# Causal attention with relative positions: scores made twice, the second time with keys on partitions, and the output steps of four row tiles taken together

## The chip, the cores and the metric

The kernel runs on one core of a Trainium2 chip. The metric is the device time of one execution in microseconds (us), the median of several executions. A profiled execution gives the trace from which all rows below are taken.

## The reference, cut to what matters

The input is 8 sequences of 512 rows and 128 channels. After a layer norm each sequence goes through one causal attention layer with 16 heads of 8 channels, and then through six layers of windowed attention and a feed-forward layer, which the change leaves alone.

```python
scores = jnp.einsum('bhqd,bhkd->bhqk', Qh, Kh)
rel_k = rel_k_table[clip(k - q, -2, 2) + 2]
scores = (scores + jnp.einsum('bhqd,qkd->bhqk', Qh, rel_k)) / sqrt(8)
scores = jnp.where(causal, scores, -1e9)
attn = softmax(scores)
out = jnp.einsum('bhqk,bhkd->bhqd', attn, Vh) + jnp.einsum('bhqk,qkd->bhqd', attn, rel_v)
x = out @ W_o + b_o + x
```

For a causal row all keys that lie two or more places back share one table row, so the "far" scores are plain products with a shifted key bias. The key at the row itself and the one before it ("near") are computed apart, elementwise.

## The kernel before, in words

`relative_attention` gives each engine a program of its own; they meet in semaphores, and the order of the work is written out by hand. The loop is over 8 sequences `s` (a hardware loop, `Fori`). P is 128, TPS = 4 row tiles `qt` of 128 queries, NG = 4 groups of G = 4 heads, PAIRS = 8 pairs of heads.

- **Projection part of a sequence.** TensorE turns the input (L450), ScalarE copies it (`a_xT`, L510), TensorE multiplies by padded weights for queries and keys, eight chunks `c` of 512 columns (L460). ScalarE splits each into two parts (L517, L519) and VectorE joins them to `a_qkT` (L598), in which a head owns 32 partitions. Between chunks 1 to 4 `near_products` (L376, L377) makes the near keys and values, to which VectorE adds biases (L589, L590).
- **Pair part.** 32 items `n`: row tile `qt` outside, pair of heads inside. For an item TensorE writes a bf16 mask over the last 128 or 129 columns of both heads (L388) and adds the scores of 128 queries against 128(qt+1) keys, one head in 32 rows of the array, the two heads in two such row tiles (L393). VectorE takes both maxima in one reduce (`maxima`, L551) and the lesser of it and the near score (L554). ScalarE exponentiates with that as its bias (L495). TensorE turns the weights 128x128 at a time (`turn_weights`, L406), VectorE copies one head's out of PSUM (L629), ScalarE the other's (L531), and TensorE multiplies by the values (`values`, L421), a head's output in 32 columns of the array. `scores` runs two items ahead, `values` one behind.
- **Output part**, once for each row tile, spread among the pairs of the next tile: `copy_sums` (L505), `turn_sums` (L433), `normalize` (L563 to L569), `turn_output` (L439, L501), `project_output` (L443), `add_output` (L577). The last tile's stands by itself at the end of the sequence.

TensorE's stream is in order, so a matmul that waits holds back all behind it. `S` is four PSUM banks of scores, `PT` two, `O` and `M` one each. POOL forms the near products and near values (L357, L363, L368).

Of the kernel before, what the change touches and what calls it, by code (L numbers as in the profile page):

```python
# [20 lines left out]
F32 = mybir.dt.float32  # L21
# [6 lines left out]
P = 128  # L28
B, N, D = 8, 512, 128
TPS = N // P  # L30
# [21 lines left out]
C_NEAR = C_FAR + P + 1  # L52
C_PART = C_NEAR + H
NCONST = C_PART + 4


def constants():
# [24 lines left out]
    c[:, C_FAR:C_FAR + P + 1] = np.where(far, MASKED, 0.0)  # L82
    c[0, C_NEAR:C_NEAR + H] = MASKED

# [114 lines left out]
def relative_attention(nc, x, const, Wq, bq, Wk, bk, Wv, bv, Wo, bo, rel_k, rel_v, state, total, rank):  # L199
# [8 lines left out]

    with ExitStack() as ctx:
# [17 lines left out]


# [4 lines left out]
        sumsT = sb("a_sumsT", [P, NG, P])  # L233
# [4 lines left out]
        far_max = sb("a_far_max", [P, 2, H])  # L238
        nm = sb("a_nm", [P, 2, H])
        d01 = sb("a_d01", [P, 2, H])  # L240
        p01 = sb("a_p01", [P, 2, H])
        p_sum = sb("a_p_sum", [P, H])
        pv_near = sb("a_pv_near", [P, 2, D])
        probs = sb("a_probs", [P, 4, N])
        probsT = sb("a_probsT", [P, 2, 2, N])
        num = sb("a_num", [P, D])
        den = sb("a_den", [P, H])
        rden = sb("a_rden", [P, H])
        on = sb("a_on", [P, D])
        oT = sb("a_oT", [P, P])  # L250
        S = ctx.enter_context(nc.psum_tensor("a_S", [P, 4, 512], F32))
        PT = ctx.enter_context(nc.psum_tensor("a_PT", [P, 2, 512], F32))
        O = ctx.enter_context(nc.psum_tensor("a_O", [P, NG, P], F32))

# [5 lines left out]
        far_mask = rank["mask_bf"][:, C_FAR - C_MQ:C_FAR - C_MQ + P + 1]  # L260

        par_in, zeroed = sem("a_par_in"), sem("a_zeroed")
        bias_made = sem("a_bias_made")
        xa_in, xo_in = sem("a_xa_in"), sem("a_xo_in")
        seq_done = sem("a_seq_done")
        turned = sem("a_turned")
        xT_ready = sem("a_xT_ready")
        state_made = sem("a_state_made")
        proj = sem("a_proj")
        split_ready = sem("a_split_ready")  # L270
        qkT_ready = sem("a_qkT_ready")
        near_mm = sem("a_near_mm")
        near_ready = sem("a_near_ready")
        prods = sem("a_prods")
        s01_ready = sem("a_s01_ready")
        sm_ready = sem("a_sm_ready")
        scored = sem("a_scored")
        far_maxed = sem("a_far_maxed")
        nm_ready = sem("a_nm_ready")
        exped = sem("a_exped")  # L280
        flipped = sem("a_flipped")
        flip_dve, flip_act = sem("a_flip_dve"), sem("a_flip_act")
        summed = sem("a_summed")
        sums_out, sums_turned = sem("a_sums_out"), sem("a_sums_turned")
        d01_ready, p01_ready = sem("a_d01_ready"), sem("a_p01_ready")
        pool_chain = sem("a_pool_chain")
        fin = sem("a_fin")
        on_T, oT_ready, y_mm = sem("a_on_T"), sem("a_oT_ready"), sem("a_y_mm")
# [22 lines left out]
        NPAIR = TPS * PAIRS  # L311

        def region(qt):
            return (0, P, 1) if qt == 0 else (P * qt - 1, P + 1, 0)

        @block.sync
        def _(sp):
            def load_xa(s):
                sp.dma_start(xa[:], normed[:, bass.ds(s, 1), :, :].rearrange("p a t d -> p (a t) d")).then_inc(xa_in, 16)

            def load_xo(s):
                sp.dma_start(xo[:], x[bass.ds(s, 1), :, :].rearrange("a (t p) d -> p (a t) d", p=P)).then_inc(xo_in, 16)

            load_xa(0)
            load_xo(0)
            with sp.Fori(1, B) as s:

                sp.wait_ge(turned, s)
                load_xa(s)
                sp.wait_ge(seq_done, s * TPS + 1)  # L330
                load_xo(s)

        PAR = 16 * (4 * (2 + 3 * G) + 3 + 1 + 4 + 2)

        @block.gpsimd
        def _(pool):
            pool.memset(xT[:, 0:1], 0.0).then_inc(zeroed, 1)
            pool.memset(va[:, :, :, HA:HA + 1], 1.0).then_inc(zeroed, 1)
            pool.memset(va[:, :, :, HA + 1:], 0.0).then_inc(zeroed, 1)
            pool.wait_ge(par_in, PAR)  # L340
            for i in range(2):
                for r in range(3):
                    pool.tensor_tensor(kv_bias[:, i, r, :].rearrange("p (h d) -> p h d", h=H),
                                       bias[:, 1 + i, :].rearrange("p (h d) -> p h d", h=H),
                                       bc(rel[:, i, r, :], 1, H), ALU.add).then_inc(bias_made, 1)
# [3 lines left out]
            with pool.Fori(0, B) as s:  # L349
                pool.wait_ge(xT_ready, s + 1)  # L350
                pool.tensor_copy(state[:, bass.ds(s, 1), :], xT[:].unsqueeze(1)).then_inc(state_made, 1)
                pool.wait_ge(xo_in, 16 * s + 16)
                pool.tensor_tensor(xo[:], xo[:], bc(bias[:, 3, :], 1, TPS), ALU.add).then_inc(bias_made, 1)
# [4 lines left out]
                for qt in range(TPS):  # L358
                    u = s * TPS + qt

                    pool.wait_ge(p01_ready, u + 1)
                    for i in range(2):
                        pool.tensor_tensor(pv_near[:, i, :].rearrange("p (h d) -> p h d", h=H),  # L363
                                           near[:, 3 + i, qt, :].rearrange("p (h d) -> p h d", h=H),
                                           bc(p01[:, i, :], 2, HA), ALU.mult).then_inc(pool_chain, 1)
                    pool.tensor_tensor(p_sum[:], p01[:, 0, :], p01[:, 1, :], ALU.add).then_inc(pool_chain, 1)
                    pool.wait_ge(pool_chain, 4 * u + 2)
                    pool.tensor_tensor(pv_near[:, 0, :], pv_near[:, 0, :], pv_near[:, 1, :], ALU.add).then_inc(pool_chain, 1)  # L368

        @block.tensor  # L370
        def _(pe):
            def near_products(s, qt):

                if qt >= 2:
                    pe.wait_ge(near_ready, 6 * (s * TPS + qt - 1))
                pe.matmul(S[:, 2 + qt % 2, 0:3 * D], xT[:, 1 + P * qt:1 + P * (qt + 1)], w_all[:], start=True, stop=True)  # L376
                pe.matmul(PT[:, qt % 2, 0:2 * D], xT[:, P * qt:P * (qt + 1)], w_all[:, D:3 * D],  # L377
                          start=True, stop=True).then_inc(near_mm, 1)

            def scores(s, n):  # L380

                qt, pr = divmod(n, PAIRS)
                lo, width, skip = region(qt)

                if n >= 2:
                    pe.wait_ge(exped, 2 * (s * NPAIR + n - 1))
                for j in range(2):
                    pe.matmul(S[:, 2 * (n % 2) + j, lo:lo + width], rank["id_bf"][:], far_mask[:, skip:],  # L388
                              start=True, stop=False, skip_group_check=True)
                for j in range(2):  # L390
                    h = 2 * pr + j
                    g, r = h // G, 32 * (h % G)
                    last = pe.matmul(S[:, 2 * (n % 2) + j, 0:P * (qt + 1)], qkT[r:r + 32, 0, g, P * qt:P * (qt + 1)],  # L393
                                     qkT[r:r + 32, 1, g, 0:P * (qt + 1)], start=False, stop=True,
                                     skip_group_check=True)
                last.then_inc(scored, 1)

            def turn_weights(s, n):
                qt = n // PAIRS
                for j in range(2):  # L400

                    pe.wait_ge(exped, 2 * (s * NPAIR + n) + j + 1)
                    if n:
                        pe.wait_ge((flip_dve, flip_act)[j], s * NPAIR + n)
# [3 lines left out]
                    last.then_inc(flipped, 1)  # L408

            def values(s, n):  # L410
                qt, pr = divmod(n, PAIRS)
                if qt and pr == 0:
                    pe.wait_ge(sums_out, s * TPS + qt)
                for j in range(2):
                    pe.wait_ge((flip_dve, flip_act)[j], s * NPAIR + n + 1)

                for kt in range(qt + 1):
                    for j in range(2):
                        h = 2 * pr + j
                        r = 32 * (h % G)  # L420
                        last = pe.matmul(O[r:r + 32, h // G, :], va[:, kt, h, :],  # L421
# [1111 lines left out]
```

## Time and profile before

| | |
|---|---|
| runs of before | 4333.78, 4345.29, 4352.34 us, median 4345.29 |
| profiled execution | 4335.39 us, its span 4333.6 us |
| mean granted TensorE clock in it | 0.948 |
| busy in the span | TensorE 91%, VectorE 80%, ScalarE 55%, POOL 55% |

A span is the time from the first to the last instruction. A granted clock of 1.00 is TensorE at 2.4 GHz, 0.50 at 1.2 GHz. A row of the timeline gives the start, the length from the first start to the last end, the engine, the line and how many equal instructions were merged (x2). TensorE's matmuls overlap, so the distance from one start to the next tells more than the length of one. Float32 matmuls that are no transposes appear as two records each. A row of the windows gives the stretch, its length, the busy time and count of PE, PEld, DVE, ACT and POOL, the granted clock, the DMA share and GB/s.

### The profile page before, as it was taken

To read this page: it belongs to the slowest core of one execution; us is meant where nothing else is said; L and a number is where in the kernel's file an instruction comes from. 1 tells how busy PE (TensorE), PEld (TensorE's weight loads), DVE (VectorE), ACT (ScalarE), POOL (GpSimd) and SP (SyncE) were. 2 spreads that over 40 slices of the span, in tenths; PEclk is the share of its full clock that TensorE was granted. 3 is DMA by queue.
4 is the path that set the end of the run, shared out by engine and by line. 5 is a ranking of instruction groups with operands and counts; after the bars stand their busy time and mean duration, and the time that the engine had idled before them with its cause. 6 is when DMAs were issued, how large, how long until landed. Compare 5 with 4: busy or idle time off the path is not lost.

```text
span 4333.6 us, 175276 instructions
## 1 busy us (share of the span) xinstructions
PE 3951.8 (91%) x69760; PEld 3066.8 (71%) x69760; DVE 3471.0 (80%) x7786; ACT 2363.6 (55%) x4549; POOL 2364.7 (55%) x2932
## 2 busy tenths in 40 slices
PE   4999889699998899988999989999889998899998
PEld 2666656577876677865778757877667777578775
DVE  4676676699996898967899769999688986799886
ACT  2666565456663566644566535665356654365652
POOL 1110110278781677844787618777257874387770
PEclk8888888799999999999999999999999999999999
DMA  2000000022220222211222202222112221122220
GB/s 44 6 5 5 10 5 2 28 65 57 61 57 30 52 58 60 56 51 29 62 55 60 50 25 65 60 58 60 33 47 60 56 61 53 26 58 61 57 55 20
DMA packets 155083, 190.91 MB, mean 44 GB/s; under 512 B 56390, under 2 KB 77892, under 8 KB 153540
## 3 DMA queue, kind: packets, MB, share of 16 engines
q1 hardware_dynamic: 154308, 180.20, 16.5%
q8 instruction: 532, 8.72, 0.9%
q14 instruction: 243, 1.99, 0.2%
HBM read 22.54 MB, written 2.10 MB: 6 GB/s over the span
## 4 chain that ended last, share of the span: by engine, by line
PE 72%; DVE 5%; issue 3%; ACT 0%; POOL 0%; DVEq 0%; DMA 0%; SPq 0%; ACTq 0%; POOLq 0%
PE PS L989 17%; PE PS L975 9%; PE PS L1109 9%; PE PS L976 7%; PE PS L977 7%; PE PS L1013 7%; PE PS L999 7%; PE PS L1159 3%; PE PS L1103 2%; PE PS L1137 1%; PE PS L1125 1%; PE PS L1130 1%; DVE ss L1386 1%; DVE m L1391 0%; DVE t L1379 0%
## 5 line engine op out<-in xcount | busy, mean ns | idle before, releaser
L927 POOL TENSOR_TENSOR t<-t 128x1024 f32<-128x1024 f32 x384 | 908.5, 2372 | 332.0 <-DVE t L1381 331.4
L1211 ACT ACTIVATE va<-PS 128x512 f32<-128x512 f32 x384 | 230.3, 600 | 1001.1 <-PE PS L977 1000.9
L932 POOL TENSOR_TENSOR t<-t,rn 128x1024 f32<-128x1024 f32 x384 | 724.0, 1906 | 31.0 <-POOL rn L137 31.0
L975 PE MATMUL PS<-w_hi,xh 128*128 128x512 f32 x1152 | 520.2, 452 | 74.6 <-DVE xl L823 63.0
L1379 DVE TENSOR_TENSOR t<-PS,rope 128x512 f32<-128x512 f32 x768 | 523.1, 681 | 25.3 <-ACT sq L1242 24.7
L1242 ACT ACTIVATE sq<-PS 128x512 f32<-128x512 f32 x768 | 455.7, 593 | 32.9 <-PE PS L977 12.6
L977 PE MATMUL PS<-w_lo,xh 128*128 128x512 f32 x1152 | 465.2, 404 | 8.1 <-issue 8.1
L989 PE MATMUL PS<-constants,t 128*128 128x128 f32 x3072 | 449.6, 281 | 23.4 <-POOL t L932 21.3
L976 PE MATMUL PS<-w_hi,xl 128*128 128x512 f32 x1152 | 465.4, 404 | 2.0 <-issue 2.0
L1386 DVE TENSOR_REDUCE ss<-sq 128x16 f32<-128x1024 f32 x384 | 448.4, 1209 | 0.0
L989 PEld LDWEIGHTS PS<-constants,t 128*128 128x128 f32 x3072 | 358.2, 143 | 72.5 <-POOL t L932 24.6
L1109 PE MATMUL PS<-oT,w_out 128*128 128x128 f32 x3072 | 394.2, 281 | 4.3 <-ACT oT L1211 4.2
L1013 PE MATMUL PS<-vs,shared 64*32 64x65 f32 x18432 | 341.4, 229 | 40.7 <-issue 40.7
L1109 PEld LDWEIGHTS PS<-oT,w_out 128*128 128x128 f32 x3072 | 357.5, 191 | 23.1 <-ACT oT L1211 5.8
L495 ACT ACTIVATE a_probs<-a_S,a_nm 128x512 f32<-128x512 f32 (+3 forms) x512 | 241.8, 524 | 216.4 <-DVE a_nm L554 158.7
L1013 PE MATMUL PS<-va,shared 64*32 64x65 f32 x6144 | 343.3, 229 | 16.7 <-issue 16.7
L999 PEld LDWEIGHTS PS<-kT,qT 64*32 64x32 f32 x24576 | 273.1, 105 | 116.8 <-issue 93.0
L1013 PEld LDWEIGHTS PS<-vs,shared 64*32 64x32 f32 x18432 | 268.6, 107 | 113.8 <-issue 113.7
L999 PE MATMUL PS<-kT,qT 64*32 64x64 f32 x24576 | 340.2, 224 | 6.4 <-issue 5.9
L975 PEld LDWEIGHTS PS<-w_hi,xh 128*128 128x128 f32 x1152 | 221.8, 193 | 155.1 <-issue 77.0
L363 POOL TENSOR_TENSOR a_pv_near<-a_near,a_p 128x128 f32<-128x128 f32 x64 | 24.7, 408 | 556.0 <-ACT a_p L540 556.0
L1380 DVE TENSOR_TENSOR t<-PS,rope 128x256 f32<-128x256 f32 x768 | 318.8, 415 | 0.0
(162 smaller groups left out, 8830.2 us busy)
## 6 DMA issues: line engine op xcount, KB each, us to landing
vs<-va SPq DMA_DIRECT2D x768, 130.0 KB
vs<-va SPq DMA_DIRECT2D x768, 65.0 KB
t<-in_L_ffn_Wqkv SPq DMA_DIRECT2D x6, 1536.0 KB, 6.6
w_out<-in_L_ffn_Wo SPq DMA_DIRECT2D x6, 512.0 KB, 7.7
a_normed<-in_L_attn_x SPq DMA_DIRECT2D x8, 256.0 KB, 5.2
a_xa<-a_normed SPq DMA_DIRECT2D x8, 256.0 KB, 2.7
a_xo<-in_L_attn_x SPq DMA_DIRECT2D x8, 256.0 KB, 3.0
out<-total SPq DMA_DIRECT2D x8, 256.0 KB, 3.5
```

The source lines that it names most:

```text
L927: pool.tensor_tensor(mine[:, i, :], mine[:, i, :], t2[:, i, :], ALU.add).then_inc(done, 1)
L932: pool.tensor_tensor(h, h, bc(rn[:, H * i:H * (i + 1)], 2, HB), ALU.mult).then_inc(done, 1)
L975: pe.matmul(out, hi, w_hi, start=True, stop=False)
L976: pe.matmul(out, lo, w_hi, start=False, stop=False)
L977: return pe.matmul(out, hi, w_lo, start=False, stop=True)
L989: last = pe.transpose(PS[:, bank, P * j:P * (j + 1)], source(j), ident)
L999: last = pe.matmul(PS[W * w:W * (w + 1), 2 + par, 2 * W * pair:2 * W * (pair + 1)], qT[rows, pair, W * w:W * (w + 1)], kT[rows, t % 2, pai ...
L1013: last = pe.matmul(PS[W * w:W * (w + 1), (0, 2)[c] + par, HB1 * (pair % 4):HB1 * (pair % 4 + 1)], pT[rows, pair, W * w:W * (w + 1)], v, st ...
L1109: last = pe.matmul(PS[:, 4, 0:P], w_out[:, pair, :], oT[:, pair, :], start=(pair == 0), stop=(pair == PAIRS - 1))
L1242: act.activation(sq[:, i, 512 * c:512 * (c + 1)], PS[:, bank, :], ACT.Square).then_inc(done, 1)
L1379: dve.tensor_tensor(o1, src, bc(rope[:, 2 * i, t, :], 1, 8), ALU.mult)
L1386: dve.tensor_reduce(ss[:, H * i:H * (i + 1)], sq[:, i, :].rearrange("p (h d) -> p h d", h=H), X, ALU.add).then_inc(ss_made, 1)
```

## The change

1. Scores are made twice. `natural_scores` makes them as before (128 queries on partitions), but one head at a time through two PSUM banks, for the maxima alone; 64 items in a sequence. VectorE reduces each by itself.
2. For each group of four heads, `negate_maxima` takes the lesser of the negated maximum and the near score, `turn_maxima` turns these with four transposes, and VectorE copies them to a row layout (`neg_t`).
3. `turned_scores` makes the scores a second time, keys on partitions, for all later queries: tile `kt` has 512 - 128 kt columns, four heads in four banks. It writes the mask, adds the negated maximum with a product of a selecting matrix (`pick`), and adds the scores. ScalarE exponentiates it without a bias, and `values` uses the weights as they are, four heads in the four column tiles. The transposes of L406 and the copies of L629 and L531 are gone.
4. The output part is done once for a sequence, for four row tiles together, during the next sequence's projection; `near_products` come two chunks later.
5. The loops over sequences are unrolled.

```diff
-            def turn_weights(s, n):
...
-                    for kt in range(qt + 1):
-                        last = pe.transpose(PT[:, j, P * kt:P * (kt + 1)],
-                                            probs[:, 2 * (n % 2) + j, P * kt:P * (kt + 1)], ident)
...
+            def natural_scores(s, g, i):
+                qt, r = divmod(i, G)
...
+                if g or i >= 2:
+                    pe.wait_ge(far_maxed, item(s, g, i) - 1)
+                pe.matmul(S[:, i % 2, lo:lo + width], rank["id_bf"][:], far_mask[:, skip:],
+                          start=True, stop=False, skip_group_check=True)
+                pe.matmul(S[:, i % 2, 0:P * (qt + 1)], qkT[rows, 0, g, P * qt:P * (qt + 1)],
+                          qkT[rows, 1, g, 0:P * (qt + 1)], start=False, stop=True, skip_group_check=True).then_inc(nat_mm, 1)
...
+            def turned_scores(s, g, kt):
+                n = N - P * kt
+                mask = min(n, P + 1)
+                if kt == 0:
+                    pe.wait_ge(neg_turned, group(s, g) + 1)
+                for pair in range(2):
...
+                    for r in heads:
+                        pe.matmul(ST[:, r, 0:mask], rank["id_bf"][:], far_mask_t[:, 0:mask],
+                                  start=True, stop=False, skip_group_check=True)
+                    for r in heads:
+                        rows = slice(32 * r, 32 * (r + 1))
+                        pe.matmul(ST[:, r, 0:n], pick[rows, :], neg_t[rows, g % 2, P * kt:N],
+                                  start=False, stop=False, skip_group_check=True)
...
+                for i in range(ITEMS):
+                    natural_scores(s, 0, i)
+                turn_maxima(s, 0)
+                pe.wait_ge(near_ready, 6 * TPS * (s + 1))
+                for g in range(NG):
+                    for kt in range(TPS):
+                        turned_scores(s, g, kt)
+                        if kt:
+                            values(s, g, kt - 1)
+                        elif g:
+                            values(s, g - 1, TPS - 1)
+                        if g + 1 < NG:
+                            for i in CHUNKS[kt]:
+                                natural_scores(s, g + 1, i)
+                    if g + 1 < NG:
+                        turn_maxima(s, g + 1)
+                values(s, NG - 1, TPS - 1)
```

`CHUNKS` is 6, 6, 4 and 0 items. ITEMS is 16: four row tiles of four heads.

TensorE before, one item of the last row tile (`a_PT` turned weights, `a_S` scores, `a_O` sums):

```order
L406 MATMUL a_PT<-constants,a_probs 128x128 [waits a_flip_dve,a_exped]
L406 MATMUL a_PT<-constants,a_probs 128x128 x3
L402 REGISTER_ALU
L406 MATMUL a_PT<-constants,a_probs 128x128 [waits a_flip_act,a_exped]
L406 MATMUL a_PT<-constants,a_probs 128x128 x3
L386 ISA
L388 MATMUL a_S<-mask_bf,id_bf 128x129 [waits a_exped]
L388 MATMUL a_S<-mask_bf,id_bf 128x129
L393 MATMUL a_S<-a_qkT 128x512 x2
```

TensorE now, step `kt` = 1 of the first group and the start of its six natural items (`a_ST` turned scores, `a_neg_t` the maxima):

```order
L409 MATMUL a_ST<-mask_bf,id_bf 128x129 [waits a_exped]
L409 MATMUL a_ST<-mask_bf,id_bf 128x129
L413 MATMUL a_ST<-a_neg_t,a_pick 128x384 x2
L417 MATMUL a_ST<-a_qkT 128x384 x2
L426 MATMUL a_O<-a_probs,a_va 32x512 [waits a_exped]
L426 MATMUL a_O<-a_probs,a_va 32x512 x3
L385 MATMUL a_S<-mask_bf,id_bf 128x129 [waits a_far_maxed]
L387 MATMUL a_S<-a_qkT 128x256
L385 MATMUL a_S<-mask_bf,id_bf 128x129 [waits a_far_maxed]
L387 MATMUL a_S<-a_qkT 128x256
L385 MATMUL a_S<-mask_bf,id_bf 128x129 [waits a_far_maxed]
L387 MATMUL a_S<-a_qkT 128x384
```

Before, TensorE went on to the values of the pair before; now each natural item is a mask and one head's scores, and waits for the reduce of two items earlier.

VectorE before, in the pair part, where each item had a reduce of two heads and a copy:

```order
L551 TENSOR_REDUCE a_far_max<-a_S 128x2 [waits a_scored]
L554 SCALAR_TENSOR_TENSOR a_nm<-a_far_max,a_sm 128x2 [waits a_far_maxed]
L626 ISA
L629 COPY a_probsT<-a_PT 128x256 [waits a_summed,a_flipped]
L550 REGISTER_ALU
```

VectorE now, from the first group of a sequence on:

```order
L574 TENSOR_REDUCE a_far_max<-a_S 128x1 [waits a_nat_mm] x16
L579 TENSOR_REDUCE a_s<-a_prod 128x64 [waits a_prods] x2
L581 TENSOR_TENSOR a_s<-a_s,constants 128x16 [waits a_s01_ready]
L583 TENSOR_TENSOR a_sm<-a_s 128x64 [waits a_sm_ready]
L585 TENSOR_SCALAR a_sm<-a_sm 128x64 [waits a_sm_ready]
L593 SCALAR_TENSOR_TENSOR a_neg<-a_far_max,a_sm 128x16 [waits a_far_maxed,a_sm_ready]
L599 TENSOR_TENSOR a_d<-a_s,a_neg 128x4x4 [waits a_neg_made]
L599 TENSOR_TENSOR a_d<-a_s,a_neg 128x4x4
L604 CAST a_neg_t<-a_M 128x512 [waits a_neg_mm]
```

The near scores (L579 to L585), which came before the first reduce, now stand behind sixteen of them and ahead of the handing over of the first maxima.

## Rows read from the trace of the kernel before

**Rows 1.** The page: granted clock in 40 slices of 108 us, in tenths

```profile
PEclk8888888799999999999999999999999999999999
```

**Rows 2.** Windows: one sequence; then everything behind the attention (busy, counts, clock)

```profile
147.40:243.00 95.60, 87.59 (x693) 59.62 (x690) 65.45 (x161) 57.20 (x126) 10.79 (x21) 0.86 0.02 5
822.50:4333.60 3511.10, 3245.37 (x64256) 2586.20 (x64256) 2927.65 (x6388) 1905.59 (x3541) 2272.97 (x2754) 0.97 0.21 52
```

**Rows 3.** Timeline: where the parts of a sequence begin

```profile
248.15 1.06 PE L450 MATMUL a_PT<-constants,a_xa 128*128 128x128 f32 x4
...
266.66 0.34 PE L388 MATMUL a_S<-mask_bf,id_bf 128*128 128x128 bf16 x2 [2.51 <-DVE a_qkT L598]
...
339.42 0.60 ACT L505 ACTIVATE a_sumsT<-a_O 128x512 f32<-128x512 f32 x1 [1.13 <-PE a_O L421]
...
340.06 1.08 PE L433 MATMUL a_M<-constants,a_sumsT 128*128 128x36 f32 x8 [0.69 <-ACT a_sumsT L505]
...
343.73 1.06 PE L450 MATMUL a_PT<-constants,a_xa 128*128 128x128 f32 x4
```

**Rows 4.** Windows cut where the granted clock changes, one sequence

```profile
253.10:266.60 13.50, 10.34 (x29) 4.93 (x27) 11.94 (x33) 9.61 (x15) 3.65 (x3) 1.00 0.00 0
266.60:287.10 20.50, 18.95 (x101) 11.37 (x102) 12.21 (x39) 9.33 (x33) 1.36 (x4) 0.50 0.00 0
287.10:341.80 54.70, 52.97 (x550) 40.32 (x548) 40.60 (x89) 35.02 (x76) 4.09 (x12) 1.00 0.00 0
```

**Rows 5.** Timeline at the high clock: masks, scores, values, and the reduce released

```profile
318.70 0.28 PE L388 MATMUL a_S<-mask_bf,id_bf 128*128 128x129 bf16 x2
...
318.90 0.50 PE L393 MATMUL a_S<-a_qkT 32*128 32x512 f32 x2
...
319.33 0.85 PE L421 MATMUL a_O<-a_probsT,a_va 128*32 128x128 f32 x12
319.45 1.23 DVE L551 TENSOR_REDUCE a_far_max<-a_S 128x2 f32<-128x1024 f32 x1
```

**Rows 6.** Timeline at the low clock: the same places

```profile
270.50 0.47 PE L393 MATMUL a_S<-a_qkT 32*128 32x128 f32 x2
...
270.90 0.69 PE L406 MATMUL a_PT<-constants,a_probs 128*128 128x128 f32 x2
...
282.33 0.43 PE L388 MATMUL a_S<-mask_bf,id_bf 128*128 128x129 bf16 x2
...
282.69 0.58 PE L393 MATMUL a_S<-a_qkT 32*128 32x256 f32 x2
```

**Rows 7.** Groups of one shape, 50 to 823 us (busy, mean ns | idle before)

```profile
L551 DVE TENSOR_REDUCE a_far_max<-a_S 128x2 f32<-128x512 f32 x64 | 44.1, 690 | 25.1 <-PE a_S L393 24.8
L357 POOL TENSOR_TENSOR a_prod<-a_near 128x512 f32<-128x512 f32 x16 | 27.7, 1750 | 71.9 <-DVE a_va L590 71.9
L551 DVE TENSOR_REDUCE a_far_max<-a_S 128x2 f32<-128x256 f32 x64 | 27.2, 425 | 26.2 <-PE a_S L393 25.2
L495 ACT ACTIVATE a_probs<-a_S,a_nm 128x512 f32<-128x512 f32 x128 | 81.1, 684 | 50.2 <-PE a_PT L406 29.4 <-DVE a_nm L554 20.6
L629 DVE COPY a_probsT<-a_PT 128x128 f32<-128x128 f32 x64 | 18.7, 292 | 18.0 <-PE a_PT L406 17.3
```

**Rows 8.** A group of the high-clock stretch, 287.1 to 341.8 us

```profile
L406 PE MATMUL a_PT<-constants,a_probs 128*128 128x128 f32 x137 | 20.5, 281 | 0.4 <-ACT a_probsT L531 0.3
```

**Rows 9.** Timeline of VectorE: the near scores' chain

```profile
266.45 1.26 DVE L609 TENSOR_REDUCE a_s<-a_prod 128x64 f32<-128x512 f32 x2
...
268.22 0.20 DVE L617 TENSOR_SCALAR a_sm<-a_sm 128x64 f32<-128x64 f32 x1
```

**Rows 10.** Timeline of a windowed layer: matmuls in eight tiles of 64 rows and 32 columns

```profile
1500.07 0.27 PE L1013 MATMUL PS<-vs,shared 64*32 64x65 f32 x5
...
1500.21 0.25 PE L1013 MATMUL PS<-vs,shared 64*32 64x65 f32 x5
```

More of the change, by code:

```diff
@@ L310, in relative_attention, with group, item, step @@
         block = ctx.enter_context(nc.Block())
-        NPAIR = TPS * PAIRS
-        def region(qt):
-            return (0, P, 1) if qt == 0 else (P * qt - 1, P + 1, 0)
+        NC = 2 * NG
+        ITEMS = TPS * G
+        CHUNKS = (range(0, 6), range(6, 12), range(12, 16), range(16, 16))
+        PAR = 16 * (4 * (2 + 3 * G) + 3 + 1 + 4 + 2)
+        def group(s, g):
+            return s * NG + g
+        def item(s, g, i):
+            return group(s, g) * ITEMS + i
+        def step(s, g, kt):
+            return group(s, g) * TPS + kt
+        def per_head(h):
+            return h.rearrange("p (h d) -> p h d", h=H)
+        def per_tile_head(h):
+            return h.rearrange("p t (h d) -> p t h d", h=H)
         @block.sync
         def _(sp):
[L318 to L333, printed above, removed]
+            for s in range(B):
+                if s:
+                    sp.wait_ge(turned, s)
+                sp.dma_start(xa[:], normed[:, s, :, :]).then_inc(xa_in, 16)
+                if s:
+                    sp.wait_ge(seq_done, s)
+                sp.dma_start(xo[:], x[s].rearrange("(t p) d -> p t d", p=P)).then_inc(xo_in, 16)
         @block.gpsimd
         def _(pool):
-            pool.memset(xT[:, 0:1], 0.0).then_inc(zeroed, 1)
-            pool.memset(va[:, :, :, HA:HA + 1], 1.0).then_inc(zeroed, 1)
-            pool.memset(va[:, :, :, HA + 1:], 0.0).then_inc(zeroed, 1)
+            pool.memset(xT[:, 0:1], 0.0).then_inc(made, 1)
+            pool.memset(va[:, :, :, HA:HA + 1], 1.0).then_inc(made, 1)
+            pool.memset(va[:, :, :, HA + 1:], 0.0).then_inc(made, 1)
             pool.wait_ge(par_in, PAR)
@@ L378, in near_products @@
+                pe.matmul(ST[:, b, 0:2 * D], xT[:, P * qt:P * (qt + 1)], w_all[:, D:3 * D],
                           start=True, stop=True).then_inc(near_mm, 1)
[L380 to L396, printed above, removed]
@@ L410, in values @@
[L410 to L421, printed above, removed]
-                                         probsT[:, n % 2, j, P * kt:P * (kt + 1)], start=(kt == 0), stop=(kt == qt),
-                                         skip_group_check=True)
-                last.then_inc(summed, 1)
@@ new lines, in values @@
+            def values(s, g, kt):
+                n = N - P * kt
+                pe.wait_ge(exped, G * (step(s, g, kt) + 1))
+                if kt == 0 and group(s, g):
+                    pe.wait_ge(sums_out, group(s, g))
+                for r in range(G):
+                    last = pe.matmul(O[32 * r:32 * (r + 1), P * kt:N], va[:, kt, G * g + r, :], probs[:, kt % 2, r, 0:n],
+                                     start=(kt == 0), stop=(kt == TPS - 1), skip_group_check=True)
+                last.then_inc(val_mm, 1)
@@ L431, in turn_sums @@
+            def turn_sums(s):
+                pe.wait_ge(sums_out, group(s, NG))
                 keep = ident.rearrange("p (h c) -> p h c", h=G)[:, :, 0:HA + 1]
-                for g in range(NG):
-                    last = pe.matmul(M[:, 36 * g:36 * (g + 1)], sumsT[:, g, :], keep, start=True, stop=True,
-                                     skip_group_check=True)
+                for qt in range(TPS):
+                    for g in range(NG):
+                        last = pe.matmul(ST[:, qt, 36 * g:36 * (g + 1)], sumsT[:, g, P * qt:P * (qt + 1)], keep,
+                                         start=True, stop=True, skip_group_check=True)
@@ L435, in turn_sums, with turn_output @@
                 last.then_inc(sums_turned, 1)
-            def turn_output(s, qt):
-                pe.wait_ge(fin, 4 * (s * TPS + qt) + 4)
-                pe.transpose(M[:, TURNED], on[:], ident).then_inc(on_T, 1)
-            def project_output(s, qt):
-                pe.wait_ge(oT_ready, s * TPS + qt + 1)
-                pe.matmul(M[:, Y], oT[:], wo[:], start=True, stop=True).then_inc(y_mm, 1)
+            def turn_output(s):
+                pe.wait_ge(fin, 4 * s + 4)
+                for qt in range(TPS):
+                    last = pe.transpose(ST[:, qt, TURNED], on[:, qt, :], ident)
+                last.then_inc(on_T, 1)
@@ L445, in _, with project_output @@
+            def project_output(s):
+                pe.wait_ge(oT_ready, s + 1)
+                for qt in range(TPS):
+                    last = pe.matmul(ST[:, qt, Y], oT[:, qt, :], wo[:], start=True, stop=True)
+                last.then_inc(y_mm, 1)
             pe.wait_ge(bias_made, 8)
-            pe.wait_ge(zeroed, 3)
-            with pe.Fori(0, B) as s:
+            pe.wait_ge(made, 5)
+            for s in range(B):
+                if s:
+                    turn_sums(s - 1)
                 pe.wait_ge(xa_in, 16 * s + 16)
@@ L480, in _ @@
-                values(s, NPAIR - 1)
-                turn_sums(s, TPS - 1)
-                turn_output(s, TPS - 1)
-                project_output(s, TPS - 1)
+                project(s, 0)
+                if s:
+                    turn_output(s - 1)
+                project(s, 1)
+                if s:
+                    project_output(s - 1)
+                project(s, 2)
+                if s:
+                    pe.wait_ge(seq_done, s)
+                for c in range(3, NC):
+                    if c - 3 < TPS:
+                        near_products(s, c - 3)
+                    project(s, c)
@@ new lines, in turn_output, with weights @@
+            def turn_output(s):
+                act.wait_ge(on_T, s + 1)
+                act.activation(oT[:], ST[:, :, TURNED], ACT.Copy).then_inc(oT_ready, 1)
+            def weights(s, g, kt):
+                n = N - P * kt
+                for r in range(G):
+                    act.wait_ge(st_mm, G * step(s, g, kt) + r + 1)
+                    if step(s, g, kt) >= 2:
+                        act.wait_ge(val_mm, step(s, g, kt) - 1)
+                    act.activation(probs[:, kt % 2, r, 0:n], ST[:, r, 0:n], ACT.Exp, scale=SCALE_A).then_inc(exped, 1)
@@ L643, in _ @@
+            normalize(B - 1)
+            add_output(B - 1)
+            dve.wait_ge(seq_done, B)
             dve.wait_ge(state_made, B)
```

393 lines of the change are left out of this document (181 added, 212 removed).

## The prediction

> **What bounds the kernel now.** The page's clock line shows a mean of 0.8 in the first 7 slices (756 us) and 0.9 behind them [rows 1]: the attention part is the slower stretch, and the change touches nothing else. The windows give its size: a sequence lasts 95.60 us, TensorE is busy in 87.59 of them, VectorE in 65.45, ScalarE in 57.20, and what comes after the attention takes 3511.10 us, which I keep [rows 2]. The timeline then cuts a sequence [rows 3]: projection part 248.15 to 266.66 (18.5 us), pairs to 339.42 (72.8), the last output part to 343.73 (4.3). Cut at the changes of the granted clock, the pairs are two stretches [rows 4]: 20.50 us at 0.50 (1.2 GHz; all pairs of the first row tile), in which TensorE is shown busy for 18.95, and 54.70 us at 1.00 (2.4 GHz), busy 52.97. So TensorE is the bound through the pairs, and VectorE follows it. Two things decide the change: how long TensorE's new stream is, item by item with its waits, and at which clock it runs.
>
> **Prices.** At the high clock two masks take 0.20 from the first's start to the scores' start (318.70 to 318.90), two heads' scores of 512 columns 0.43 to the next matmul (318.90 to 319.33), and the reduce starts 0.55 after the scores (319.45) [rows 5]. One column a cycle is 0.053 us for 128, so scores of 384, 256 and 128 columns take 0.37, 0.31, 0.25 and one mask instead of two 0.14. In that 0.25 only 0.05 is columns: about 0.2 is paid at the change from 32-row scores to the next full-array matmul, whichever the width. VectorE needs 690 ns for 512 columns and 425 for 256; with the 292 of a 128-column copy that is 292, 425, 558, 690 [rows 7]. I take 0.06 us from the reduce's end back to TensorE.
>
> **The change, a group of four heads.** (a) *Removed*: turning the weights, 137 recorded transposes of L406 in the high stretch alone [rows 8]. 128 columns fed as float32 take twice the 0.053 of one column a cycle, about 0.11 each, so 15 of the 54.70 us. I don't subtract them but rebuild the sequence from its new parts.
>
> (b) *Natural items.* TensorE's own time is mask 0.14 plus 0.25, 0.31, 0.37, 0.43: 0.39 to 0.57, 7.7 us for the 16 of a group. But each waits for the reduce two items earlier. A bank's round is 0.14 + (0.37, 0.43, 0.49, 0.55) + (0.29, 0.43, 0.56, 0.69) + 0.06 = 0.86, 1.05, 1.24, 1.44, and two banks share it: 0.43, 0.52, 0.62, 0.72, or 9.2 us a group. VectorE in this loop is not full either: its reduces sum to 7.9. Bounds: TensorE's 7.7 below and 9.2 above.
>
> (c) *Turned scores.* A step has two pairs of heads, each two masks 0.20, two products with the maxima, and two scores 0.43, 0.37, 0.31, 0.25. The products are 32-row tiles; if the two heads run together they cost their columns alone, 0.22, 0.17, 0.11, 0.11: in all 0.85, 0.74, 0.62, 0.56 a pair, 5.5 us a group. Bound: if these don't pair, a second set of columns, some +5 us a sequence (+40).
>
> (d) *Values.* 12 records of 128 columns in two column tiles last 0.85 us to the last end [rows 5]; less a tail of about 0.2 that is 0.11 for two records side by side, 0.22 for the two records of a matmul. Four heads side by side then take 0.88, 0.66, 0.44, 0.22 for the four widths, with 4 x 0.1 for the change of shape 2.6 us a group. That four column tiles do run together I take from the windowed layers: ten records of 65 columns between 1500.07 and 1500.21 [rows 10], 0.014 each, less than the 0.027 that one alone needs for its columns. Bound: two at a time, +2.2 a group, +70 in all.
>
> (e) *Handing over the maxima.* Four transposes at 0.11, 0.2 to VectorE, a copy of 512 (0.69) and the return: 1.4 us. TensorE has nothing else in its stream there (`CHUNKS` ends with 0), so it is on the path. Scores of the next group wait for it. In the first group the near scores stand ahead of it on VectorE: 266.45 to 268.42 is this chain today (two reduces of 1.26, then three small ones to 268.22 + 0.20) [rows 9], so 2.0 + 0.2 for the negation + 1.4 = 3.6. POOL's products before it, 2 x 1.75 [rows 7], are made during the natural items and are hidden.
>
> The group is 9.2 + 5.5 + 2.6 + 1.4 = 18.7, three times 56.1. Ahead stand the first natural items and their handing over, 9.2 + 3.6 = 12.8; the fourth group has no natural items, 5.5 + 2.6 + 0.5 = 8.6.
>
> (f) *Output part.* `turn_sums` has 32 records, 8 of which last 1.08 today [rows 3]; less the tail, 0.11 each at the high clock: 3.6. With the copy ahead of it (0.65), the projection part 18.5 and 1.0 for the output's chain inside it: 23.7. Today projection and output part are 22.8.
>
> (g) *At nothing.* ScalarE: four exponentials of 684 ns [rows 7] are 2.7 us in the widest step, and a step with its natural items lasts over 4. POOL's chain for the near values starts in the last group and has the output's projection to run under. Loads and the later `near_products` lie under other work; unrolling I put at 0, gain at most 1 us a sequence.
>
> **Sum at the high clock**: 12.8 + 56.1 + 8.6 + 23.7 = 101.2 us, 5.6 more than 95.6, eight times 45: 4335 + 45 = 4380.
>
> **The clock.** Today it falls as TensorE idles before the first pairs (266.66 follows a wait of 2.51 [rows 3]) and stays at 0.50 for all the 128-column pairs [rows 4]. The change puts at this very place sixteen items that carry a mask and one head's scores in 0.43 to 0.72 us where a pair carries two, with TensorE waiting in each, and then a wait of 3.6 us. At low clock two masks take 0.36 (282.33 to 282.69) and a score of 128 columns 0.40 (270.50 to 270.90) [rows 6]; with 0.107 for each further 128 an item is 0.65, 0.76, 0.86, 0.97, 13.0 a group instead of 9.2. Turned steps become 9.7 (+4.2), values +2.3, handing over +0.5: a group +10.8, the first natural part +4.3, the last group +6.6. In the pair part this is 0 (high throughout) to 43.3 (low throughout). I choose low for the first natural part and one and a half groups, because today's clock needed 20.5 us of steady pairs to come back, while the natural stretches, up to 13 us a group at the low clock, cut the steady work up; it is a choice between ends far apart: 4.3 + 16.2 = 20.5, so 121.7 a sequence. 26.1 x 8 = 209: 4335 + 209 = 4544 for the profile, 4550 with the 10 by which the median stands above it.
>
> The Trainium skill, page "TensorE: Matmul & The Clock Gate", Part 4, says that PE-mode transposes do not count as activity for the clock gate. Here 137 of them ran at a granted 1.00 between 287.10 and 341.80, between other matmuls [rows 8]. By the rule alone the removal would help the clock, which is the second case below; the row doesn't decide.
>
> **Rivals.** *High clock throughout* (4380 to 4390, 0.13): for it, the turned steps are denser streams than today's pairs. Against it, [rows 4]'s low stretch was shown 92% busy.
>
> *Low throughout the pair part* (101.2 + 43.3 = 144.5, 4335 + 391 = 4726, 0.15): the natural items recur in three of four groups and could hold it down each time.
>
> *Not slower* (4297, 0.08): the items go at VectorE's pace. If a reduce started as the one before ended, 0.29 to 0.69, the 64 items would take less: with a mean of 0.41 for 0.57, 10.4 us less a sequence. At the high clock 101.2 - 10.4 = 90.8, 38 us below today. Below 0.48 us a mean item (0.57 - 5.6/64, rounded) this decides. Against it: two banks and the 0.55 from score to reduce [rows 5].
>
> *Another price* of the bounds, at the mixed clock (0.02 faster or same; the rest is slower).
>
> The Trainium skill, page "TensorEngine Tiling (Array Packing)", Key Properties, says that a change of tiling mode drains TensorE. The change alternates full array, 32-row and 32-column tiles far oftener. The page gives no time; this trace gives about 0.2 behind scores and 0.1 behind values, and these are already in (b) to (d).
>
> **How the numbers follow.** Mixed clock 0.62, high 0.13, low 0.15, not slower 0.08, others 0.02. The predicted time is that of the likeliest, 4550. The range takes the high case's 4380 and the low one's 4720; what lies beyond them is the not-slower case, the low case's upper half and part of the bounds. A measurement here tells about 0.5% (22 us) from no change, so: slower 0.91, same 0.04, faster 0.05.
>
> **What would show it.** Right: a period near 121 us; natural items spaced 0.43 to 0.72 (or 0.65 to 0.97 at granted 0.50), waiting for L574; four values of 512 columns within 0.9 us; 3.6 us idle before the first turned step; a clock of 0.50 from the first natural item into the second group; TensorE's busy share lower, VectorE's about the same. Wrong: a clock that rises within the first natural part (then 4380), natural items without waits, values in two turns (+70), products with the maxima one after another (+40), or exponentials as the releaser of turned steps, which I priced at nothing.

## The result, and the profile after

The changed kernel takes 4755.66 us (median of 4 runs, 4753.74 to 4757.11) against 4348.82 of before: ratio 1.094, 95% interval 1.091 to 1.097. That is above the range of 4380 to 4720; it is 30 us above the second rival (low clock throughout the pair part, 4726).

The page's clock line of the changed kernel, to be held against [rows 1]; a slice is 119 us:

```profile
PEclk7555555555699999999999999999999999999999
```

The windows of one sequence, of the stretch at the high clock in it, and of the one at the low clock that follows (columns as in [rows 2]):

```profile
343.60:490.90 147.30, 135.10 (x547) 66.68 (x548) 51.37 (x124) 38.57 (x87) 9.04 (x8) 0.56 0.01 4
349.80:366.90 17.10, 12.38 (x44) 6.70 (x42) 11.11 (x35) 9.38 (x14) 3.45 (x3) 1.00 0.10 32
366.90:496.60 129.70, 122.22 (x502) 59.54 (x502) 40.10 (x88) 29.19 (x73) 5.59 (x6) 0.50 0.00 1
```

A sequence lasts 147.3 us instead of 95.6, and eight times 51.7 is 414, nearly all of the 421 us by which the spans of the two profiles differ (4754.5 against 4333.6; the medians differ by 407). TensorE has 547 recorded matmuls in it where it had 693, is busy for 135.1 instead of 87.6, and VectorE and ScalarE are needed less (51.4 and 38.6). The granted clock is 1.00 in 17.1 us of the projection part alone; it falls 1.4 us after the first natural item (366.90), which had followed 3.23 us of idling, and stays at 0.50 for 129.7 us, through the next sequence's first projections.

The timeline of TensorE, from the first natural items to the next sequence:

```profile
365.50 0.23 PE L385 MATMUL a_S<-mask_bf,id_bf 128*128 128x128 bf16 x1 [3.23 <-DVE a_qkT L568]
365.66 0.32 PE L387 MATMUL a_S<-a_qkT 32*128 32x128 f32 x1
365.91 0.23 PE L385 MATMUL a_S<-mask_bf,id_bf 128*128 128x128 bf16 x1
...
380.33 1.12 PE L395 MATMUL a_M<-constants,a_neg 128*128 128x128 f32 x4 [2.89 <-DVE a_neg L593]
382.28 0.38 PE L409 MATMUL a_ST<-mask_bf,id_bf 128*128 128x129 bf16 x2 [0.83 <-issue]
382.58 0.79 PE L413 MATMUL a_ST<-a_neg_t,a_pick 32*128 32x512 f32 x2
383.18 0.63 PE L417 MATMUL a_ST<-a_qkT 32*128 32x512 f32 x2
383.74 0.40 PE L409 MATMUL a_ST<-mask_bf,id_bf 128*128 128x129 bf16 x2
...
388.42 0.29 PE L385 MATMUL a_S<-mask_bf,id_bf 128*128 128x129 bf16 x1
388.64 0.58 PE L387 MATMUL a_S<-a_qkT 32*128 32x256 f32 x1
389.15 0.40 PE L409 MATMUL a_ST<-mask_bf,id_bf 128*128 128x129 bf16 x2
...
391.68 1.94 PE L426 MATMUL a_O<-a_probs,a_va 128*32 128x512 f32 x8
393.55 0.29 PE L385 MATMUL a_S<-mask_bf,id_bf 128*128 128x129 bf16 x1
...
410.45 0.40 PE L409 MATMUL a_ST<-mask_bf,id_bf 128*128 128x129 bf16 x2 [0.79 <-DVE a_neg_t L604]
...
439.23 0.40 PE L409 MATMUL a_ST<-mask_bf,id_bf 128*128 128x129 bf16 x2 [0.79 <-DVE a_neg_t L604]
...
468.01 0.40 PE L409 MATMUL a_ST<-mask_bf,id_bf 128*128 128x129 bf16 x2 [0.79 <-DVE a_neg_t L604]
...
483.61 7.04 PE L435 MATMUL a_ST<-constants,a_sumsT 128*128 128x36 f32 x32 [0.72 <-ACT a_sumsT L524]
490.46 1.09 PE L458 MATMUL a_S<-constants,a_xa 128*128 128x128 f32 x4
```

Scores and products with the maxima leave one record for each matmul, so `x2` is two heads; the values (`x8` is four heads), the sums, the projections and the unread float32 matmuls of e4, e5 and e9 below leave two.

The reader is to see three things. Between the handings over, TensorE never idles for VectorE: a 256-column item takes 0.73 us (388.42 to 389.15) by TensorE's own time, not by the reduce. The groups follow each other 28.8 us apart (410.45, 439.23, 468.01). And in the pair part all scores and all products with the maxima are over 32 rows of the array (`32*128`); masks, values and the turning of the maxima are over 128. Summed over the records of the three groups from 382.3 to 468.0, matmuls over 32 rows are 57.4 of 98.7 us; in the stretch of before that ran at 1.00, 287.1 to 341.8, they are 9.4 of 62.8.

### The profile page after: what moved, and what is told of

Read it like the earlier page. It is cut to its first block, busy times and chain, and to the rows that moved or that the text cites. A ratio compares the mean times of both kernels' runs of the same rounds, so it can differ in the third digit from the quotient of the medians.

```text
span 4754.5 us, 168913 instructions
## 1 busy us (share of the span) xinstructions
PE 4330.7 (91%) x68608; PEld 3120.8 (66%) x68608; DVE 3359.6 (71%) x7475; ACT 2213.3 (47%) x4238; POOL 2345.4 (49%) x2836
## 4 chain that ended last, share of the span: by engine, by line
PE 66%; DVE 5%; issue 3%; ACT 0%; POOL 0%; DVEq 0%; DMA 0%; SPq 0%; ACTq 0%; POOLq 0%
PE PS L994 15%; PE PS L980 8%; PE PS L1114 8%; PE PS L982 7%; PE PS L981 7%; PE PS L1018 7%; PE PS L1004 6%; PE PS L1164 3%; PE PS L1108 2%; PE PS L1142 1%; PE PS L1130 1%; PE PS L1135 1%; DVE ss L1391 1%; DVE m L1396 0%; DVE t L1384 0%
## 5 line engine op out<-in xcount | busy, mean ns | idle before, releaser
L574 DVE TENSOR_REDUCE a_far_max<-a_S 128x1 f32<-128x384 f32 (+3 forms) x512 | 251.6, 491 | 443.3 <-PE a_S L387 442.5
L518 ACT ACTIVATE a_probs<-a_ST 128x256 f32<-128x256 f32 (+3 forms) x512 | 196.0, 434 | 735.7 <-PE a_ST L417 735.6
L1247 ACT ACTIVATE sq<-PS 128x512 f32<-128x512 f32 x768 | 455.6, 593 | 35.4 <-PE PS L982 15.4
L356 POOL TENSOR_TENSOR a_pv_near<-a_near,a_p 128x512 f32<-128x512 f32 x16 | 16.8, 1072 | 862.3 <-ACT a_p L545 862.3
```

What stands on the lines that cost most here:

```text
L1247: act.activation(sq[:, i, 512 * c:512 * (c + 1)], PS[:, bank, :], ACT.Square).then_inc(done, 1)
```

## The experiments

The first theory was the prediction's: the clock is lost in TensorE's waits and thin natural items. Its rivals were the unrolling, and the added work whatever the clock. The first four runs ask that. Where an expectation says theory A, it is that matmuls over 32 rows don't hold the clock, or that full-array columns do; it came up after e3. Ratios, with their 95% intervals, are to the kernel before, run on the same chip.

**e1: the kernel before, unrolled.**

```diff
-            with pe.Fori(0, B) as s:
+            for s in range(0, B):
```

(the same on the other engines)

> The kernel before with its loops over sequences unrolled and nothing else. Clock theory (the loss is TensorE at 1.2 GHz through the pair part): no change, 4335 to 4350 us. Rival theory (unrolled code costs, or moves the work at the seams): up to 1% slower; were the whole loss from it, 4750.

4351.24 us, ratio 1.006 (1.004 to 1.008). So unrolling accounts for some 0.6 of the 9.4 percent (at most 0.8), and that goes with the clock: with TensorE's order unchanged, its windows show a low stretch of 27.3 us at the first pairs, where [rows 4] has 20.5. Others have up to 34.5 us, and all but the first have periods (from one sequence's start to the next's) of 97 to 102 us for 95.6.

```profile
362.40:389.70 27.30, 25.67 (x139) 16.40 (x140) 14.99 (x49) 12.13 (x39) 1.36 (x4) 0.50 0.00 1
```

**e2 and e3: the changed kernel with unread matmuls around its first natural items, and behind all natural items.** The `fill(1)` stands behind each natural item, in e2 of the first group alone.

```diff
+                    pe.matmul(M[:, 0:width], rank["id_bf"][:], rank["mask_bf"][:, 0:width], start=True, stop=True, ...)
...
+                fill(24)
                 pe.wait_ge(qkT_ready, NC * (s + 1))
...
+                fill(1)
...
+                fill(24)
                 turn_maxima(s, 0)
```

> The changed kernel, with matmuls whose result nobody reads (256 bf16 columns, 0.11 us each at 2.4 GHz) put into TensorE's waits around the first group's natural items: 24 in the wait for the last queries and keys, one behind each of the 16 items, 24 in the wait for the first maxima. Clock theory: the clock, which falls at the first natural items, stays at 1.00 there; if the three later groups of natural items can hold it, the period is near 101 us (total near 4385); if they lose it by themselves it falls at the first chunk of the second group's items and the total is 4690 to 4740. Rival theory (32-row matmuls don't carry the clock, or the added work is what costs): no change or slower, 4755 to 4790.

> As the one before, with such a matmul behind every natural item of all four groups. Clock theory: granted clock near 1.00 in the whole pair part, period 99 to 105 us, total 4365 to 4420: most of the loss of 410 us is the clock, and 20 to 75 us are the work itself. Rival theory (the added work costs what it costs, whatever the clock): 64 more matmuls a sequence add 7 to 14 us each sequence, 4810 to 4870.

e2: 4745.32 us, 1.097 (1.093 to 1.100). e3: 4825.70 us, 1.114 (1.112 to 1.117). Both miss the clock theory's hope. e2 lies between the two ranges written down for it (up to 4740, and from 4755), and e3 lands on the rival's number. Windows of e3 in one sequence:

```profile
373.50:394.00 20.50, 18.11 (x85) 10.68 (x85) 13.22 (x40) 9.38 (x14) 4.19 (x3) 1.00 0.08 26
394.00:407.60 13.60, 13.60 (x47) 6.66 (x48) 7.67 (x17) 0.00 (x0) 0.00 (x0) 0.50 0.00 1
407.60:414.40 6.80, 5.97 (x39) 3.37 (x37) 2.42 (x7) 2.06 (x4) 0.00 (x0) 1.00 0.00 0
414.40:530.50 116.10, 112.33 (x491) 52.24 (x489) 28.15 (x60) 27.02 (x69) 4.71 (x5) 0.50 0.00 1
```

The filling keeps the clock at 1.00 through the wait. It falls all the same at 394.00, 4.4 us into natural items that follow each other without a gap (from 389.59), and TensorE is shown busy for all of the next 13.60 us at a granted 0.50. So waits are not what takes the clock here or holds it down. It rises in the second filling of 24 full-array matmuls (402.72 to about 407.8), and falls again 6.8 us later, behind a wait of 0.83 us, the first turned step and six natural items of the second group; in e2, where these six have no filling, it falls at the same place. That led to the new theory (A): columns that pass 32 rows of the array do not hold the clock.

**e4: the kernel before with unread full-array matmuls in two waits.**

```diff
+                    pe.matmul(M[:, 416:512], ident, ident[:, 0:96], start=True, stop=True, skip_group_check=True)
...
+                fill(14)
                 pe.wait_ge(qkT_ready, 2 * NG * s + 2 * NG)
...
                 scores(s, 1)
+                fill(12)
```

> The kernel before, with matmuls whose result nobody reads (96 float32 columns into an unused part of bank M, 0.16 us each at 2.4 GHz): 14 in the wait for the last queries and keys, 12 in the wait for the first exponentials. Clock theory: the clock no longer falls there, the first row tile's pairs take 10 to 14 us instead of 20.5, so 6 to 10 us less a sequence, total 4265 to 4300. Rival theory (128-column pairs lose the clock by themselves): it falls a few us later, total 4330 to 4370.

4284.89 us, 0.990 (0.988 to 0.992). The windows of its first row tile's pairs, and of a sequence from 148.7 us to its last output part:

```profile
163.00:177.00 14.00, 13.47 (x113) 9.14 (x114) 9.67 (x34) 8.44 (x30) 1.16 (x4) 1.00 0.00 0
148.70:234.00 85.30, 81.46 (x734) 59.09 (x732) 63.82 (x159) 54.93 (x123) 8.96 (x18) 1.00 0.00 0
```

The low stretch of [rows 4] is gone, and the pairs take 14 us for 20.5. The period is some 91.4 us, 4 less and not the 6 to 10 expected: an unread matmul takes 0.22 us (14 of them in 3.10), not 0.16, so the second filling overruns its wait.

**e5: the same, the unread matmuls over 32 rows.** One line differs from e4:

```diff
-                    pe.matmul(M[:, 416:512], ident, ident[:, 0:96], ...)
+                    pe.matmul(M[:, 416:512], ident[0:32, :], ident[0:32, 0:96], ...)
```

> The kernel before with the same unread matmuls as in the run that held its clock (4285 us), the same number, columns and places, but over 32 rows of the array instead of 128. Theory A (matmuls over 32 rows do not hold the clock): it falls at the first pairs again, the first row tile's pairs take about 20 us, total 4345 to 4375 (the filling now costs what it overruns, 1 to 2 us a sequence). Theory B (any stream of matmuls holds it; in the changed kernel it is TensorE's waits): 4280 to 4290 again.

4390.77 us, 1.013 (1.009 to 1.018). Its windows, the filled wait and what follows, and two rows of its timeline there:

```profile
375.60:378.70 3.10, 3.10 (x28) 3.08 (x28) 2.96 (x5) 1.58 (x3) 1.25 (x1) 1.00 0.00 0
378.70:412.90 34.20, 34.20 (x184) 23.76 (x184) 15.97 (x51) 12.97 (x42) 1.36 (x4) 0.50 0.00 0
```

```profile
375.62 3.48 PE L382 MATMUL a_M<-constants 32*128 32x96 f32 x28
...
380.09 5.43 PE L382 MATMUL a_M<-constants 32*128 32x96 f32 x24
```

TensorE is busy without a gap through the wait, as in e4, but the clock falls 3.1 us into the filling (378.70) and stays down for 34.2 us of unbroken work. Only the rows differ, and within the filling no tile shape changes: theory A against B is settled for such matmuls. The size was 16 us above what was expected: the low stretches are longer than before's 20.5, and the second filling takes 5.4 us at the low clock. Its last 27.4 us (385.5 to 412.9) are the ordinary first pairs, with their transposes, at 0.50 and without a gap; in e4 the same pairs stayed at 1.00. So the clock at which such a stretch is entered counts too.

**e6: the changed kernel with scores and maxima products over all 128 rows.** It leaves out the separation of the heads.

```diff
-                pe.matmul(S[:, i % 2, 0:P * (qt + 1)], qkT[rows, 0, g, P * qt:P * (qt + 1)],
-                          qkT[rows, 1, g, 0:P * (qt + 1)], ...)
+                pe.matmul(S[:, i % 2, 0:P * (qt + 1)], qkT[:, 0, g, P * qt:P * (qt + 1)],
+                          qkT[:, 1, g, 0:P * (qt + 1)], ...)
...
-                        pe.matmul(ST[:, r, 0:n], pick[rows, :], neg_t[rows, g % 2, P * kt:N], ...)
+                        pe.matmul(ST[:, r, 0:n], pick[:], neg_t[:, g % 2, P * kt:N], ...)
```

(turned scores likewise)

> The changed kernel with natural scores, products with the maxima and turned scores taken over all 128 rows of the array (so each head gets the sum of its group's four scores: the output is not the reference's); columns, items, waits and VectorE's work stay, the products of two heads no longer run side by side, and the changes between full and 32-row tiles are gone. Theory A: the granted clock is 1.00 in nearly the whole pair part, period 94 to 102 us, total 4330 to 4400. Theory B: natural items still wait for VectorE, so the clock is lost there as before, total 4600 or more.

4416.17 us, 1.019 (1.015 to 1.023), period 106 to 109. Windows: first the later part of the pairs with the next output part, then the first natural items and what follows them:

```profile
413.50:478.30 64.80, 57.55 (x445) 36.71 (x444) 24.51 (x60) 24.51 (x65) 3.62 (x4) 1.00 0.00 1
393.00:413.50 20.50, 16.12 (x56) 9.91 (x56) 11.57 (x29) 2.17 (x4) 2.40 (x2) 0.50 0.00 0
```

The clock is 1.00 for 64.8 us in which nearly all of the 48 natural items of the later groups still run, and TensorE is busy for less of them (57.55, 89%) than in the changed kernel's low stretch (94%); here it does wait for VectorE's reduces, 3.9 us in all. The clock is lost only around the first natural items and their 3 us waits (17 to 24 us a sequence), which probably is why the time lies 16 us above the range. The edit changes two things at once: the rows, and how often the tile shape changes. It alone can't tell them apart; e5 can.

**e7: the changed kernel, output unchanged, held up by full-array columns.** The `fill(2, ...)` stands behind each natural item; the fillings of e2 ahead of the first items and maxima are there too.

```diff
-                        pe.matmul(ST[:, r, 0:n], pick[rows, :], neg_t[rows, g % 2, P * kt:N],
+                        pe.matmul(ST[:, r, 0:n], pick[:, r, :], neg_t[:, g % 2, P * kt:N],
...
+                fill(2, 192 + 64 * qt)
...
                         turn_maxima(s, g + 1)
+                        fill(9, bank=S[:, 0, :])
```

> The changed kernel, output unchanged, with the selecting product over all 128 rows (one head at a time) and two unread full-array matmuls behind each natural item (2 x 192 to 2 x 384 columns, growing with the item), 24 and 24 and 9 in the waits around the first maxima and 9 in the later ones. Theory A: enough full-array columns in every stretch hold 1.00, period 110 to 120 us although TensorE is given some 35 percent more columns; total 4450 to 4530, 230 to 300 less than the changed kernel. Theory B: more work at the low clock, 4850 to 5000.

4599.15 us, 1.059 (1.055 to 1.064). Some 150 us less than the changed kernel, with more columns, but 69 us above the range. In its profile the sequence from 448.04 to 572.22 takes 124.2 us, 116.1 of them at 1.00:

```profile
454.60:570.70 116.10, 112.89 (x737) 64.39 (x736) 48.65 (x117) 36.03 (x83) 7.80 (x7) 1.00 0.02 6
```

but others lasted up to 139.5 and have stretches of up to some 30 us at 0.50 (216.3 to 245.5, busy without a gap): the columns hold the clock only narrowly. Its timeline at 1.00 also gives two prices that the kernel after never shows at that clock:

```profile
394.12 0.44 PE L422 MATMUL a_ST<-a_qkT 32*128 32x384 f32 x2
394.49 1.06 PE L431 MATMUL a_O<-a_probs,a_va 128*32 128x512 f32 x8
395.49 0.23 PE L390 MATMUL a_S<-mask_bf,id_bf 128*128 128x129 bf16 x1
```

**e8: natural items for the first group alone.** The other three groups use its maxima.

```diff
-                        if g + 1 < NG:
-                            for i in CHUNKS[kt]:
-                                natural_scores(s, g + 1, i)
-                    if g + 1 < NG:
-                        turn_maxima(s, g + 1)
```

> The changed kernel with natural items and maxima for the first group of four heads only; the other three groups use that group's maxima (their shift is not their own maximum). It prices 48 items and three handings over, and leaves TensorE a stream without waits in three groups. Theory A (32-row matmuls don't count): the clock stays at 0.50 all the same, 14.2 us less a group, period 104 to 106 us, total 4405 to 4425. Theory B (waits for VectorE keep it low): it rises in the second group, period 70 to 80 us, total 4130 to 4220.

4402.00 us, 1.015 (1.010 to 1.019), period 104.4, as theory A has it (the total is 3 us under its range). A window of turned steps and values without any natural item or wait for VectorE:

```profile
402.00:448.00 46.00, 46.00 (x254) 18.67 (x254) 0.00 (x0) 21.54 (x55) 0.00 (x0) 0.50 0.00 1
```

Busy for all of 46.00 us and at 0.50 throughout. So neither natural items nor waits are needed to keep the clock down once it is low.

**e9: the kernel before with its other waits filled as well.**

```diff
+                fill(4, S[:, 3, 0:96])
                 turn_sums(s, TPS - 1)
+                fill(4, S[:, 3, 0:96])
                 turn_output(s, TPS - 1)
+                fill(1, S[:, 3, 0:96])
                 project_output(s, TPS - 1)
```

(and 3 ahead of the wait for `xT`, 12 and 8 where e4 has 14 and 12)

> The kernel before, output unchanged, with full-array unread matmuls in all its longer waits of TensorE: 12 instead of 14 ahead of the last queries and keys, 8 instead of 12 ahead of the first exponentials (each of those 12 measured 0.24 us and ran 0.8 us past the exponentials), and 4, 4, 1 and 3 in the waits of the last output part and of the next sequence's input. Theory A (full-array columns hold the clock wherever they stand): the granted clock no longer falls at a sequence's end, period 88 to 91 us instead of 92.3, total 4250 to 4275. Rival: the tail's matmuls of 36 columns lose it all the same, or the filling overruns the waits: 4275 to 4300.

4277.13 us, 0.984 (0.980 to 0.988), period 88.4, 7 less than before. Its attention part in one window:

```profile
54.20:757.00 702.80, 684.35 (x5998) 492.98 (x5996) 521.17 (x1285) 454.92 (x1005) 85.17 (x159) 1.00 0.02 5
```

The clock never falls in 702.8 us. The microseconds are 2 above the range and the period in it; the kernel before was 20 us slower on this chip than on that of e4. The gain of 1.6% over the kernel before is clear of the interval.

## Why the prediction was wrong, point by point

**What bounds the kernel: right.** TensorE's stream and its clock decided; through the pairs it waited for the others only around the first natural items and at the handings over.

**The step that failed** is "I choose low for the first natural part and one and a half groups". That put 0.50 on 20.5 us' worth of a possible 43.3; measured, it is 0.50 from the fourth natural item on, past the end of the sequence, 129.7 us without a break. I took the turned steps for steady work that brings the clock back, as today's pairs do. They are not like today's pairs: a turned step's scores and maxima products run over 32 rows, as the natural scores do, and only its masks and values over 128. With the transposes of L406 the change takes out 128-row work. e5 against e4 shows that a filling over 32 rows does not hold the clock, e2 and e3 that it falls within 7 us even where a filling had brought it back ahead of the turned steps, e8 that turned steps and values stay low by themselves, and e6 that with full rows, and so fewer changes of tile shape, nearly the same stream runs at 1.00. Whether changes of tile shape add to it is not shown. That the removed transposes carried today's clock is argued, not shown: no run took them out alone, and e6, which has none of them either, runs at 1.00 for 64.8 us. The chance of 0.15 for "low throughout" was too small, and its cause ("the natural items recur and hold it down") was at best half the right one: they are 32-row work too, but e8 stays low without them. The range also stopped at 4720, short of that case's own 4726.

**The sum of that case**, 144.5 us against 147.3, by parts of the timeline, is close partly by luck: the pair part came out 3.4 us shorter and the rest 6.2 longer. First natural items and handing over: 17.1 forecast, 16.8 measured (365.50 to 382.28). A group: 29.5, measured 28.2 for the first (no values ahead of it) and 28.8 for the others. The last group: 15.2; measured 14.9 (468.01 to about 482.9, where the sums' copy starts). Output and projection: 23.7, measured 29.9. Two terms were mis-sized there: `turn_sums` was priced at the high clock, 3.6, and takes 6.9 at the low one (483.61 to 490.46); and the projection part takes 21.9 instead of 19.5, mostly since `near_products` come later and wait for VectorE (1.49, and then 3.23 ahead of the first natural item for 2.51).

**Single prices.** At 0.50 a natural item of 256 columns was 0.76 and is 0.73; at 1.00, by the starts in e2 from 386.09 on, items of 128 take 0.41 to 0.46 where 0.43 was forecast, and the first pair of a turned step 0.87 (384.34 to 385.21) for 0.85. Four values of 512 side by side were 0.88 + 0.1, and two at a time would be 1.76 + 0.1: e7 has 1.00 (394.49 to 395.49), so all four column tiles do run at once and the +70 fell away. The forecast had this from a weak reading: 0.014 for a record of 65 columns is half of 0.027, which shows two side by side, not four (and the trace has 16 records from 1500.07 to 1500.21, not ten). The products with the maxima pair: 0.60 for two of 512 at 0.50 (382.58 to 383.18), not twice 0.43. The waits around the first handing over were there (2.89 and 0.83, for 3.6).

**The rule of the Trainium skill** on transposes, in "TensorE: Matmul & The Clock Gate", Part 4, would have made their removal good or neutral for the clock. The clock went the other way; as no run isolates it, that is no test of the rule. The same page of the Trainium skill says in Part 1, "What's actually happening", that the gate goes by how busy TensorE has been. The busy share of the profile doesn't give that: 34.20 of 34.20 us at 0.50 in e5.

**The other side.** At the low clock the pace of VectorE did not matter: the items were slower by themselves and ran without waits, which the prediction lists as a sign of being wrong. Only e6, at the high clock, shows waits for its reduces. The rival "not slower" was also summed wrongly: its reduces of 292, 425, 558 and 690 ns have a mean of 0.49 us, not 0.41, so its sequence would take some 96 us, no less than today's 95.6.

**What the change costs without its clock** is only bounded. e7 holds 1.00 for most of a sequence of 124.2 us with extra columns: 16 items' fillings, by their columns 0.16, 0.21, 0.27 and 0.32 us each, are 3.8 us a group, and the unpaired products 1.1. That leaves 124.2 - 15.4 - 4.3 = 104.5, beside the 101.2 forecast (an estimate: fillings partly lie in waits, and 6.8 us were still at 0.50). The kernel before, its clock held, takes 88.4 (e9). So of the 51.7 us lost some 43 are the clock, by this estimate, and with both clocks held the new order would still lose, not gain.

## What to carry to other kernels

Before replacing transposes or other 128-row matmuls by more 32-row ones, look at how much of the new stream is over 32 rows and at the granted clock of stretches that are already like it, and work out the time at both clocks. A low clock hands itself on: it lasted here through the next sequence's first projections. Where a stretch of full-array work is cut by waits of 1 to 3 us, unread full-array matmuls in those waits can pay (1.0% in e4, 1.6% in e9); the same over 32 rows cost 1.3% (e5).

## What the runs showed of the hardware

- Matmuls of 96 float32 columns over 32 rows, without a gap, let the clock fall from 1.00 to 0.50 where the same over 128 rows kept it (e5, e4).
- The busy share alone does not tell the clock: 100% busy at 0.50 for 34.20 us (e5) and 13.60 us (e3) and 46.00 us (e8), 89% busy at 1.00 for 64.8 us (e6).
- The same first pairs ran for 27.4 us at 0.50 in e5, without a gap, and at 1.00 in e4, where the clock was high as they began.
- Four matmuls in four tiles of 32 columns run side by side: 1.00 us for the values of four heads of 512 columns (e7).
- Unrolling alone, with TensorE's order unchanged, lengthened the low stretch at the first pairs from 20.5 to 27.3 us and more (e1). Why is open.
